# Four transformer levels on one core: a ScalarE table set is loaded by name in the six-layer stack

## The reference

```python
def attn_layer(x, Wqkv, qs, ksc, Wo):              # 16 heads of 64
    q, k, v = split(x @ Wqkv)
    q = l2norm(q) * qs;  k = l2norm(k) * ksc       # l2norm: t / max(norm(t), 1e-12)
    q, k = rotary(q), rotary(k)                    # scaled by position
    return local_attention(q, k, v) @ Wo           # windows of 32 keys, softmax
def ffn_layer(x, g, bln, W1, b1, W2, b2):
    xn = layernorm(x) * g + bln
    a, gate = jnp.split(xn @ W1 + b1, 2, -1)       # 341 each
    return a * gelu(gate) @ W2 + b2
for i in range(6):
    x = attn_layer(shift_tokens(x), ...) + x
    x = ffn_layer(shift_tokens(x), ...) + x
```

## Time and profile before

| | |
|---|---|
| median of 3 runs | 5938.94 us (5917.71 to 5954.47) |
| profiled execution | 5932.37 us, of which the span from the first to the last instruction is 5930.6 |
| TensorE's mean granted clock | 0.933 |
| busy | TensorE 87%, ScalarE 72%, VectorE 65%, GpSimd 48% |
| the two stacks | from about 1040 to 3045 us, and from about 3295 to 5338 us |

### The profile page before, as it was taken

How to read it: one execution, slowest core, us unless ns; L and a number is a source line. 1 busy time by engine, 2 the same in 40 slices (tenths; PEclk the granted TensorE clock), 3 DMA queues, 4 the chain that set the end, 5 groups by cost and what they waited for, 6 DMA issues and landing times. The chain is left out here.

```text
span 5930.6 us, 142455 instructions
## 1 busy us (share of the span) xinstructions
PE 5174.4 (87%) x49044; PEld 3529.4 (60%) x49044; DVE 3842.9 (65%) x7030; ACT 4279.4 (72%) x6551; POOL 2865.3 (48%) x3451
## 2 busy tenths in 40 slices
PE   8899965798988988998978688988989889879889
PEld 5655644466666666666655366666666666656556
DVE  2343255677777777777745577777777777755545
ACT  3343323799999999999945598999989989963442
POOL 0000023666666666666620566666666666630200
PEclk9989976899999999999979799999999999989899
DMA  1000000111111111111100111111111112110000
GB/s 40 4 1 30 1 8 27 30 34 52 39 48 38 53 38 46 45 45 46 34 14 1 46 37 47 42 45 41 50 41 42 44 34 57 34 30 18 7 22 8
DMA packets 110453, 195.51 MB, mean 33 GB/s; under 512 B 21408, under 2 KB 28848, under 8 KB 110256
## 3 DMA queue, kind: packets, MB, share of 16 engines
q1 hardware_dynamic: 110256, 192.82, 11.6%
HBM read 53.29 MB, written 1.05 MB: 9 GB/s over the span
## 5 line engine op out<-in xcount | busy, mean ns | idle before, releaser
L2671 POOL TENSOR_TENSOR stage_qk<-stage_halves 128x1024 f32<-128x1024 f32 x384 | 904.2, 2355 | 96.5 <-DVE stage_halves L2787 94.9
L2784 DVE TENSOR_TENSOR stage_halves<-stage_wide,stage_tables 128x1024 f32<-128x1024 f32 x384 | 469.4, 1222 | 505.2 <-ACT stage_square L2493 450.7
L2700 POOL TENSOR_TENSOR stage_probs<-stage_probs,stage_rsum 128x768 f32<-128x768 f32 x384 | 564.2, 1469 | 480.2 <-DVE stage_rsum L2816 467.5
L2707 POOL TENSOR_TENSOR stage_qk<-stage_qk,stage_rnorm 128x1024 f32<-128x1024 f32 x384 | 730.5, 1902 | 30.3
L2311 PE MATMUL stage_flip<-ident,stage_probs 128*96 128x128 f32 x3072 | 494.1, 286 | 236.1 <-ACT stage_probsT L2539 214.6
L2311 PEld LDWEIGHTS stage_flip<-ident,stage_probs 128*96 128x96 f32 x3072 | 354.4, 131 | 469.1 <-ACT stage_probsT L2539 266.9
L2276 PE MATMUL stage_turn<-ident,stage_qk 128*128 128x128 f32 x3072 | 516.2, 294 | 87.6 <-ACT stage_qkT L2513 87.4
L2539 ACT ACTIVATE stage_probsT<-stage_flip 96x512 f32<-96x512 f32 x768 | 451.6, 588 | 143.2 <-PE stage_flip L2311 142.9
L2276 PEld LDWEIGHTS stage_turn<-ident,stage_qk 128*128 128x128 f32 x3072 | 375.6, 149 | 255.7 <-ACT stage_qkT L2513 166.3
L2325 PEld LDWEIGHTS stage_pv<-stage_probsT,stage_v_win 96*64 96x64 f32 x12288 | 421.9, 143 | 143.3 <-issue 119.1
L2325 PE MATMUL stage_pv<-stage_probsT,stage_v_win 96*64 96x64 f32 x12288 | 502.7, 232 | 1.8 <-ACT stage_ctxT L2546 1.6
(11 more groups left out here) (301 smaller groups left out, 10389.0 us busy)
## 6 DMA issues: line engine op xcount, KB each, us to landing
stage_v_win<-stage_v SPq DMA_DIRECT2D x384, 192.0 KB, 2.5
stage_v_win<-stage_v SPq DMA_DIRECT2D x384, 128.0 KB, 2.4
stage_v_win<-stage_v SPq DMA_DIRECT2D x192, 64.0 KB, 2.2
stage_wq<-in_T_wq SPq DMA_DIRECT2D x12, 512.0 KB, 4.2
stage_wk<-in_T_wk SPq DMA_DIRECT2D x12, 512.0 KB, 4.8
stage_wv<-in_T_wv SPq DMA_DIRECT2D x12, 512.0 KB, 3.5
stage_wo<-in_T_wo SPq DMA_DIRECT2D x12, 512.0 KB, 3.5
stage_w_up<-in_L_w_up SPq DMA_DIRECT2D x8, 512.0 KB, 7.0
```

Source lines behind the costliest of these rows:

```text
L2671: nc.gpsimd.tensor_tensor(qk[:, n, :], halves[:, n % 2, 0, :], halves[:, n % 2, 1, :], ALU.add)\
L2700: nc.gpsimd.tensor_tensor(probs[:, m % 2], probs[:, m % 2], rsum[:, m % 2].to_broadcast([P, 2, 2 * HALVES, REACH]), ALU.mult)\
L2707: nc.gpsimd.tensor_tensor(heads, heads, rnorm[:, n, :].rearrange("p (h o) -> p h o", o=1).to_broadcast([P, LH, LD]), ALU.mult).then_inc(at ...
L2784: nc.vector.tensor_tensor(out[:, 0], heads, cos.to_broadcast([P, LH, LD]), ALU.mult)
```

## The change

ScalarE loads the table set `natural_log_exp_and_others` by name, which holds both Exp and Ln: once ahead of the written-out steps and the loop of each stack, and once in each step behind the third gate (`FF_CHUNKS` is 3). No arithmetic, wait or order of other instructions is altered in the text.

```diff
@@ gate(step, c), on ScalarE
                 nc.scalar.activation(gelu[0:width(c), c % 2, :], up_psum[0:width(c), 1, :], ACT.Gelu,
                                      bias=cols[0:width(c), FF_CHUNKS + c:FF_CHUNKS + c + 1]).then_inc(att["gelu"], 1)
+                if c == FF_CHUNKS - 1:
+                    nc.scalar.preload_act_table_set("natural_log_exp_and_others")
```

## The result

The changed kernel takes 5367.56 us (median of 4 runs, 5360.76 to 5375.39) against 5946.7 us (median of 4, 5917.71 to 5956.52): a ratio of 0.9034, 95% interval 0.8998 to 0.9069. That is 579 us less.

What follows compares the result with a forecast made beforehand. ScalarE was taken as late, holding up TensorE at four places a step. 90 steps at 35.3 us save 475.7, filling 20, way out 4: 500 off 5932.4, with 6.6 to the median 5440 us; range 5395 to 5610.

Steps and rivals of the forecast that it cites:

- the largest wait: TensorE at L2311 waiting for ScalarE's copy L2539: 101.1 us in the first loop, to fall to near nothing.
- the three others on ScalarE: TensorE's three smaller waits for ScalarE in the first loop, 67.7 us in all, expected to go.
- the set isn't lost: Rival: joint set lost at the loop's head, only the pair before the largest wait stays; about 5790 us, chance 4%.
- the clock doesn't sink: Rival: TensorE without pauses is granted a lower clock; at 0.82 about 6130 us; 3% together with an added load that counts.
- The rival of the second chain: TensorE waits for VectorE ahead of project(w, 1) or (w, 2); 5557 us, or 5620 at 2 us delay; chance 16%.
- late engine: ScalarE in the two loops, taken as what TensorE waits for at four places a step: 168.8 of 176 us.
- TensorE's own need of a step: Loop step of 40.24 us less 3.9 idle and 1.2 to 1.7 low clock; taken as 35.0 us.
- the thin slacks: VectorE's results reach TensorE just ahead of project(w, 1), 0.3 us, and project(w, 2), 0.4 us; 0.3 us a step added.
- The filling and the way out: Ends of each stack's pipeline: filling saves 10 us a stack, 20; way out 2 each, 4.
- the 1.7 us: Low-clock cost behind the largest wait, over two turnings and the up-projection: 0.49 + 0.46 + 0.76 us a step.
- The 1.2 us: Low-clock cost a step on TensorE, taken from the first loop's mean clock of 0.97.
- a floor of 34.6: Lower end of TensorE's need of a loop step, 34.6 to 35.1 us, taking 1.7 us for the low clock.

Runs made afterwards that it cites:

- e6: Changed kernel with the gate computing Exp in place of Gelu and the step's named load out, so no table load in the loops: 5360.4 us, ratio 0.905.
- e2: Changed kernel with two table loads put back at first_root(u, 3) alone, in front of the former largest wait: 5654.4 us, ratio 0.9521.
- e3: Changed kernel with two table loads put back at first_root(w, 2) alone, the last in the body: 5437.5 us, ratio 0.9151.
- e8: Changed kernel with the output projection cut to half, 8 of 16 matmuls: 5297.1 us, ratio 0.894.
- e9: Kernel before the change with the output projection cut to half, 8 of 16 matmuls: 5727.1 us, ratio 0.9657.
- e10: Kernel before with the joint set named at first_root(u, 3) alone, eight loads a step in place of nine: 5700.2 us, ratio 0.9621.
- e1: Changed kernel without the named load in each step, only the one ahead of the loop kept: 5900.9 us, ratio 0.9926.
- e4: Changed kernel with one load of the joint set put back ahead of first_root(u, 3): 5484.1 us, ratio 0.9224.
- e7: Changed kernel with two loads put back at all four first_root calls, ten loads a step: 5978.6 us, ratio 1.0095.

## Why the prediction came out as it did

*The mechanism held.* Both functions are served by the named set, across the loop's back edge; the largest wait and the three others on ScalarE went; the named load costs nothing (e6); the set isn't lost and the clock doesn't sink. That the place of a load decides is shown by e2 and e3, a factor of nearly five for the same two loads. The rival of the second chain did not come in, but e8 shows it 0.6 us a step away. One reading was too simple: before the change ScalarE was not *the* late engine, as e9 shows; the two waited for each other.

*The term that was mis-sized* is TensorE's own need of a step: "I take its own 35.0 and 0.3 us for what the thin slacks let through: 35.3 us a step". It measured 34.43 and 34.63, 34.53 as a mean. Over 90 steps that is 69 us more than forecast. The filling and the way out gave 19 and not 24, and together these are the 64 us by which the saving in the span (564) exceeded the forecast (500). The other 8 us of the 72 are how the medians lie to the profiled executions. Three things made it up, for the first loop:

| us a step | as forecast | measured | from |
|---|---|---|---|
| TensorE idle | 3.9 | 3.98 | (1810.98 - 1631.71) / 45 |
| resumptions and late starts | not seen | 1.0 | e10, at clock 1.00; 0.95 from the rows below |
| low clock | 1.2 to 1.7 | 0.9 | (1631.71 - 1547.87) / 45 = 1.86, less the line above |
| left by thin slacks | 0.3 | 0.0 | one wait in 45 steps after |

The trace of before bears this out. The long waits on either side of the one that the prediction read (its ends at 1839.90):

```profile
1800.54 0.64 PE L2311 MATMUL stage_flip<-ident,stage_probs 128*96 128x128 f32 x4 [2.21 <-ACT stage_probsT L2539]
1880.63 1.04 PE L2311 MATMUL stage_flip<-ident,stage_probs 128*96 128x128 f32 x4 [2.21 <-ACT stage_probsT L2539]
```

From 1800.54 to 1839.90 there is no low clock, and it takes 39.36 us: 34.43, the idle 3.98 and 0.95 for the resumptions and late starts. From 1839.90 to 1880.63, with the low clock, it takes 40.73, that is 1.37 more. So the 1.7 us, a sum of durations of operations that overlap, was too much for that step, and only 30 of the 45 steps have the low clock; but the resumptions, which no term of the prediction held, more than made up for it. The 1.2 us, from the mean clock, is the low clock alone, and it was used as if it were the whole. The 0.3 us was put in without a row that showed a wait; a slack of 0.3 us is no wait.

The second loop also lost more before (40.93) than the first, so its gain was 6.3 us a step. Its trace has the low clock behind the long wait in all 45 steps, where the first loop has it in 30. That is about 0.5 us a step, and 0.16 us is more idle time. What decides how often it comes is open. After the change the second loop takes 0.2 us a step more than the first (34.63), and there the thin slack of the prediction does show: TensorE waits 44 times, by 0.05 us at most, for VectorE's `halves` at L2259.

*The range* reached down to 34.8 us a step, while the same working had given a floor of 34.6. A range that cuts off the lower end of its own bound on one side, while it spends 170 us on the other for one rival of 16%, is badly set. Yet the floor alone would not have met it: 34.6 us a step gives 5377 us, still 9 above the time, since the floor too had no term for resumptions.

Of the two rules of the Trainium skill, neither would have helped. The Trainium skill (ScalarE: Activation LUTs, What ACT_TABLE_LOAD costs) has a drain of about 1380 ns beside each load; by it, as an estimate, the two loads of e2 would have made TensorE wait some 2.7 us longer than the 2.25 us that it waited, which two durations of 1283 ns less the slack of 0.33 explain. The Trainium skill (ScalarE activation tables: per-element evaluation and per-set limits, Table sets in the compiler and the runtime) has the loads placed by the greedy longest run; by it e1 would have one load for each pair where it has two.

## What to carry to other kernels

A table load is priced by its place: follow the in-order queue from it to the next copy that another engine awaits, and see how much slack that copy has. Two loads of 1283 ns cost 0.66 us at one place and 3.15 at another. When waits of a busy engine vanish, take its busy time as too long as well: each resumption and each stretch of low clock is counted in it, and these were 1.86 us beside 3.98 of idle time. When two engines are both at 90% and wait for each other, work taken from either shortens the step; once one is at 100%, look how near the next is before cutting more.

## What the runs showed of the hardware

- A matmul stream that resumes after a wait at full clock loses up to 0.16 us beyond the wait, as much as neighbouring operations overlap in an unbroken stream (e2: 36.80 us for 34.43 + 2.21; e4: 0.18 as a mean; e10: 0.99 for five listed waits and late starts too short to be listed).
- The low clock of 1.2 GHz showed behind waits of 2.2 us and, in e7, of 1.75 us; with waits of 1.0 us as the longest of nearly every step the loop's clock was 1.00 (e4, e10). A long wait alone doesn't bring it: it stood behind 30 and 45 of 45 such waits in the two loops of before, behind 24 of 45 in e2's first loop, and hardly ever in e7's second loop, whose clock is 1.00. What else it takes was not tried. It cost 1.37 us a time in before and 1.42 in e2.
- An active table set is kept through a hardware loop's back edge (L2533: 384 activations with 2 loads before) and from a stack into the next stage (before, a load stands at L1112 at 3070.27; after, none). A function that the active set holds is served by it; one that it doesn't hold loads its own set, even where the next function then needs another (e1, 360 pairs of loads).
